# A two-layer gated cross-attention kernel on one core: Layer 0's expert rows weighted on GpSimd, second products feature by token, new orders

## The reference, cut to what matters

```python
scores = xf @ Wr + br                                    # 8 experts, best 2 kept
router_weights = softmax(where(mask, scores, -inf))      # [token, expert]
h = gelu(einsum('td,edp->etp', xf, W1) + b1[:, None, :]) # 512 hidden features
y = einsum('etp,epd->etd', h, W2) + b2[:, None, :]
out = einsum('te,etd->td', router_weights, y)
```

## Time and profile before

| | |
|---|---|
| median of 3 runs | 4908.51 us |
| profiled execution | 4911.92 us |
| its span | 4910.1 us |
| busy: PE, DVE, ACT, POOL | 87%, 86%, 82%, 27% |
| granted TensorE clock, mean | 0.955 |
| DMA | 332.13 MB, mean 68 GB/s |

### The profile page before, as it was taken

One profiled execution on the slowest core, in us unless ns is written; L12 is line 12 of the kernel. 1 busy time (PEld: TensorE's weight loads), 2 busy tenths in 40 slices (PEclk: granted clock), 3 DMA queues, 4 the chain that ended last, 5 costly groups with the idle time before them and its releaser, 6 DMA issues. The chain is left out here.

```text
span 4910.1 us, 108232 instructions
## 1 busy us (share of the span) xinstructions
PE 4268.7 (87%) x33307; PEld 2101.1 (43%) x33862; DVE 4203.5 (86%) x22712; ACT 4014.6 (82%) x5260; POOL 1312.9 (27%) x2809
## 2 busy tenths in 40 slices
PE   5879779999798999889889999997999799998775
PEld 2435235453443535344443535444353444534222
DVE  5478998989989898998989899898989989888782
ACT  2558778989798898879879898997989699898774
POOL 3121222232223223222322333232232223122121
PEclk7889999999999999999999999999999899999887
DMA  5332232323233233323323332332333233131110
GB/s 133 77 81 64 64 69 62 79 63 80 56 77 78 60 74 72 77 59 78 79 48 77 70 88 61 77 83 53 72 73 83 53 76 76 44 70 34 36 29 21
DMA packets 356926, 332.13 MB, mean 68 GB/s; under 512 B 102659, under 2 KB 313750, under 8 KB 356310
## 3 DMA queue, kind: packets, MB, share of 16 engines
q1 hardware_dynamic: 356310, 324.86, 28.7%
HBM read 217.55 MB, written 107.13 MB: 66 GB/s over the span
## 5 line engine op out<-in xcount | busy, mean ns | idle before, releaser
L991 DVE MAX8 cand<-s 128x8 f32<-128x67 f32 (+1 forms) x12288 | 1974.9, 220 | 106.2 <-ACT s L943 92.0
L962 ACT ACTIVATE prob<-wide 128x1024 f32<-128x1024 f32 (+1 forms) x1792 | 1780.8, 1025 | 209.8 <-PE wide L656 80.9
L1077 DVE TENSOR_REDUCE part<-score 128x1 f32<-128x512 f32 x1536 | 1017.9, 677 | 213.7 <-PE score L610 134.4
L656 PE MATMUL wide<-q,k_att 128*128 128x256 bf16 (+1 forms) x6656 | 1008.8, 277 | 78.5 <-ACT prob L962 25.0
L702 PE MATMUL att<-prob,v 128*9 128x256 f32 (+1 forms) x14336 | 1044.8, 383 | 12.6 <-ACT prob L962 7.3
L943 ACT ACTIVATE s<-wide 128x1024 f32<-128x1024 f32 (+1 forms) x1024 | 844.7, 842 | 137.9 <-PE wide L630 130.9
L952 ACT ACTIVATE below<-wide 128x1024 bf16<-128x1024 f32 (+1 forms) x832 | 819.6, 1025 | 100.8 <-PE wide L656 95.9
L656 PEld LDWEIGHTS wide<-q,k_att 128*128 128x128 bf16 (+1 forms) x6656 | 557.8, 99 | 531.0 <-ACT prob L962 182.7
L610 PE MATMUL score<-k_scan,q 128*128 128x512 bf16 x1313 | 501.3, 393 | 189.7 <-DVE part L1077 114.5
L1309 POOL TENSOR_SCALAR flag<-cand,ends 128x24 bf16<-128x24 f32 x512 | 185.6, 363 | 1636.4 <-DVE ends L1016 1518.7
L678 PE MATMUL wide<-below,minus_ident 128*128 128x512 bf16 x1515 | 474.0, 388 | 137.0 <-ACT below L952 62.7
(11 more groups left out here) (169 smaller groups left out, 5257.2 us busy)
## 6 DMA issues: line engine op xcount, KB each, us to landing
k_scan<-k_stack SPq DMA_DIRECT2D x512, 150.1 KB, 3.3
k_stack<-split_b SPq DMA_DIRECT2D x576, 128.0 KB, 2.7
k_att<-k_stack SPq DMA_DIRECT2D x384, 192.0 KB, 3.6
ctxT<-in_ctx_dram SPq DMA_DIRECT2D x32, 800.5 KB, 5.8
q_stack<-split_b SPq DMA_DIRECT2D x192, 64.0 KB, 2.1
q<-q_stack SPq DMA_DIRECT2D x128, 96.0 KB
self_stack<-split_b SPq DMA_DIRECT2D x192, 64.0 KB, 2.0
k_self<-self_stack SPq DMA_DIRECT2D x64, 96.0 KB
```

The lines of the kernel that those rows point to most:

```text
L656: r = tensor.matmul(ps[0:kc, j * S:(j + 1) * S], m.k_att[kn % 3][:, j, c0:c0 + kc], rows[:, j, :], start=(j % 2 == 0), stop=(l == 0), skip ...
L962: scalar.activation(pr[0:kc, :], ps[0:kc, :], ACT.Exp, scale=SCALE).then_inc(sem["wide_done"], 1)
L991: i = vector.max(cand[:, :, c], s[:, KCUT[c]:KCUT[c + 1]])
L1077: vector.tensor_reduce(m.part[:, QT * hh + qt, c:c + 1], score[i % 2][:, :], AX.X, ALU.max).then_inc(sem["score_max"], 1)
```

## The change

Layer 0's second product is turned: w_2 is the weight operand and hid the moving one, so a result stands feature by token (128x256), and the two experts of a pair accumulate into the same bank before DVE adds it to v_acc with one plain addition. Because a token is now a column, the routing weight can't be a per-partition scalar: the eight rows of weights are written to DRAM (gate_out), read back spread over all partitions (gate_in, 128x8x256), and POOL multiplies each expert's hid rows by them (v_gate). At the end two transposes (v_turn) put the sum back token by feature into small, and x_add.v reads it there. The biases are mixed in the turned form as well. hid has four buffers instead of two. w_1 and w_2 are no longer resident: SP loads each expert's 256 KB of each into a ring of four for every batch (w_in). All five orders are new; n0 starts two steps earlier, z_score two later.

```diff
+HIDS = 4
+WBUF = 4
-                  (m.w_1[:, :, :], a["L0_ffn_W1"].rearrange("e d f -> d e f")),
-                      (m.w_2[:, e_, :, :], a["L0_ffn_W2"][e_, :, :].rearrange("(t p) d -> p t d", p=P))]
...
                     elif name == "v_w1":
-                        ps = fill(name, *key)
+                        ps, n = fill(name, *key), E * b + e
+                        q.wait_ge(w_in[n % WBUF], 32 * (n // WBUF + 1))
...
                     elif name == "v_w2":
-                        b, e = key
+                        b, pair = key
                         ps = claim(name, *key)
-                        q.wait_ge(sem["wide_done"], after("v_gelu", b, e))
-                        for t in range(QT):
+                        for e in (2 * pair, 2 * pair + 1):
+                            q.wait_ge(sem["gated"], after("v_gate", b, e))
                             for k in range(PT):
-                                r = tensor.matmul(ps[:, t * D:(t + 1) * D], hid[:, k, t * P:(t + 1) * P],
-                                                  m.w_2[:, e, k, :], start=(k == 0), stop=(k == PT - 1))
+                                r = tensor.matmul(ps[:, 0:S], w_2[:, k, :], hid[:, k, :], start=(e % 2 == 0 and k == 0),
+                                                  stop=(e % 2 == 1 and k == PT - 1))
+                    elif name == "v_turn":
+                        q.wait_ge(sem["v_added"], after("v_add", b, E // 2 - 1))
+                        turned(ps, lambda t: flat(m.r["v"].acc)[:, t * P:(t + 1) * P])
...
                     elif name == "v_add":
-                        for t in range(QT):
-                            y, w = small[:, t * D:(t + 1) * D], r.one[:, t, e:e + 1]
-                            i = vector.scalar_tensor_tensor(r.acc[:, t, :], y, w, r.acc[:, t, :], ALU.mult, ALU.add)
+                        vector.tensor_tensor(acc, small[:, 0:S], acc, ALU.add).then_inc(sem["v_added"], 1)
...
+                    elif name == "v_gate":
+                        q.wait_ge(sem["wide_done"], after("v_gelu", b, e))
+                        q.wait_ge(gate_in, 16 * (b + 1))
+                        gpsimd.tensor_tensor(hid[:, :, :], hid[:, :, :], m.gate_rows[:, e:e + 1, :].to_broadcast([P, PT, S]),
+                                             ALU.mult).then_inc(sem["gated"], 1)
...
+                    elif name == "w_in":
+                        if n >= WBUF:
+                            q.wait_ge(sem["small_full"], after("v_w2", (n - WBUF) // E, (n - WBUF) % E // 2))
+                        sync.dma_start(m.w_1[n % WBUF][:, :], a["L0_ffn_W1"][e, :, :]).then_inc(w_in[n % WBUF], 16)
+                        sync.dma_start(m.w_2[n % WBUF][:, :, :],
+                                       a["L0_ffn_W2"][e, :, :].rearrange("(t p) d -> p t d", p=P)).then_inc(w_in[n % WBUF], 16)
+                    elif name == "gate_out":
+                        q.wait_ge(sem["turned"], after("rw_copy", "v", b))
+                        sync.dma_start(d.gates[b, :, :], m.mixT["v"][0:E, :]).then_inc(gate_out, 16)
+                    elif name == "gate_in":
+                        q.wait_ge(gate_out, 16 * (b + 1))
+                        sync.dma_start(m.gate_rows[:, :, :], d.gates[b:b + 1, :, :].to_broadcast([P, E, S])).then_inc(gate_in, 16)
```

More of the change, by code:

```diff
@@ L85 @@
     pe="""
[L86 to L90, removed]
@@ L106 @@
[L106 to L110, removed]
+        rw_turn.v z_score w_k.0 mix_bias.v c1*2 pv.1 s_1 z_score s_1 z_score cut_add*2 n0 c1 n0 c1*2 n0 s_1 pv.1*2
@@ L111 @@
+        cut_add n0 pv.0 cut_add z_v c1 n0 u_turn.0 w_v.1 n0 c1 o_turn.0 n0 c1 z_qk route.z c1 z_qk n0 s_1*2 pv.1*2
+        cut_add n0 cut_add o_proj.0 w_v.1 s_1 n0*2 s_1 flag cut_add pv.1 rw_turn.z cut_add n0 c1 mix_bias.z z_moe
+        ln_turn.v c1 pv.1 c1*2 route.v n0 s_1*2 row_turn.0 pv.1 cut_add n0 pv.1 cut_add z_moe s_1 z_score n0 s_1
+        pv.1 flag cut_add n0 pv.1 cut_add v_w1 n0*2 v_w1""",
     act="""
-        exp_1 v_gelu*2 w_k_out.0 rw_copy.v c1_out mix_start.v c1_out cut*2 exp_1*2 c1_out*2 cut exp_1 row_minus.2
@@ L165 @@
+        k_scan.0*2 split_out.w_k.1 rows_out.0 k_scan.0 k_scan.1 k_att.0 x_out rows_in.0 k_scan.1 k_att.0*2 q_in.1
+        k_att.0 rows_out.1 k_att.1 rows_in.1 k_att.1 k_scan.1 k_scan.0 q_in.0 split_out.w_k.1*2 k_att.1 k_scan.1
+        split_out.z_qk k_scan.0 k_att.0 split_out.z_qk""",
 )
@@ L289, in streams @@
         of(f"{name}.z_qk", name, [("z_qk", b, n) for b in batches for n in range(2)])
-    for name in ("v_w1", "v_gelu", "v_w2", "v_add"):
+    for name in ("w_in", "v_w1", "v_gelu", "v_gate"):
         of(name, name, [(b, e) for b in batches for e in range(E)])
+    for name in ("v_w2", "v_add"):
+        of(name, name, [(b, pair) for b in batches for pair in range(E // 2)])
+    for name in ("gate_out", "gate_in", "v_turn"):
+        of(name, name, [(b,) for b in batches])
     for kind in "01vz":
@@ L365, in build @@
     smalls = T.number("pe", "small", ("b_o", "ln_turn", "row_turn", "u_turn", "o_turn", "o_proj", "route", "v_w2", "z_v",
-                                      "flag", "rw_turn", "mix_bias"))
+                                      "flag", "rw_turn", "mix_bias", "v_turn"))
     ctx = ExitStack()
@@ L422, in build @@
         m.below = [sb(f"below{n}", [P, HG * S], BF16) for n in range(2)]
-        m.hid = [sb(f"hid{n}", [P, PT, S]) for n in range(2)]
+        m.hid = [sb(f"hid{n}", [P, PT, S]) for n in range(HIDS)]
         m.u, m.rec = sb("u", [P, S]), sb("rec", [P, QT, HG])
@@ L444, in build @@
         d.rows = [dram(f"rows{l}", (B, 3, G, HG * QT, P), BF16) for l in range(3)]
+        d.gates = dram("gates_of_batch", (B, E, S))
         def semaphore(name):
@@ L453, in build @@
         prep_in, weights_in = semaphore("prep_weights_in"), semaphore("weights_in")
+        w_in = [semaphore(f"expert_weights_in{n}") for n in range(WBUF)]
+        gate_out, gate_in = semaphore("gates_out"), semaphore("gates_in")
         x_in = [semaphore(f"x_in{n}") for n in range(5)]
@@ L509, in small_drain @@
                 return "z_v_out", key
+            if name == "v_turn":
+                return "x_add", ("v", *key)
             if name == "rw_turn":
@@ L931, in _ @@
                         q.wait_ge(sem["small_full"], after("mix_bias", *key))
-                        if b:
+                        if b and kind == "v":
+                            q.wait_ge(sem["small_full"], after("v_turn", b - 1))
+                        elif b:
                             q.wait_ge(sem["x_done"], after("x_add", kind, b - 1))
@@ L1197, in _ @@
                         elif kind == "v":
-                            q.wait_ge(sem["v_added"], after("v_add", b, E - 1))
-                            vector.scalar_tensor_tensor(flat(x), flat(m.r["v"].acc), m.gates[:, 2:3], flat(x), ALU.mult,
+                            q.wait_ge(sem["small_full"], after("v_turn", b))
+                            vector.scalar_tensor_tensor(flat(x), small[:, 0:QT * D], m.gates[:, 2:3], flat(x), ALU.mult,
                                                         ALU.add).then_inc(sem["x_done"], 1)
@@ L1236, in _ @@
                             if kind == "v":
-                                q.wait_ge(sem["v_added"], after("v_add", b - 1, E - 1))
+                                q.wait_ge(sem["small_full"], after("rw_turn", kind, b - 1))
                             else:
```

209 lines of the change are left out of this document (111 added, 98 removed), and 2 rows, old and new, of the table sp.

## The result

The changed kernel takes 4991.86 us (median of 4 executions, 4984.09 to 4994.21) beside 4910.1 for the kernel before in the same session (4906.88 to 4914.14): a ratio of 1.0163 [1.0149, 1.0177], slower by 82 us and outside the range of the prediction. The profiled execution took 4994.21 us (span 4992.4), at a mean granted clock of 0.951 against 0.955.

What follows compares the result with a forecast made beforehand. PE was taken as the only bound in the experts' stretch. PE's 16 x -0.6 = -10 and start's -6 took the profiled 4911.9 to 4896, less 3.4 for the median: 4893 us; own range 4880 to 4912, wide range 4838 to 4952.

Steps and rivals of the forecast that it cites:

- Orders: New engine orders: interlocking unreadable from the trace, bounds 16.8 us per round either way, taken as 0.
- What bounds the kernel: Experts' 72 us stretch: PE alone bounds, 97% busy; a microsecond off PE there shortens the round by one.
- Second products, v_turn, biases: PE work per batch: second products save 0.8 us, transposes add 0.4, mixing biases saves 0.2; in all -0.6 us.
- DVE: Multiply-adds replaced by four additions save 3.0 us per batch where DVE is not the bound; counted as 0.
- POOL: Eight gates of 1.90 us per batch; about 2 us spare at the tightest place of PE's order; costed at 0.
- The gate's way: Two dependent DMAs through DRAM, covered by some 20 us of PE words before the first v_w2; 0.
- Weights: Per-batch weight loads in the experts' stretch fit barely; 0, or +32 us in all if late twice per batch.
- Start: Fewer initial weight loads let SP issue first keys and k_scan earlier; bounds 0 to 9 us, taken as 6 saved.
- C: Rival: gates wait behind POOL's marks, stopping PE 2.6 us per batch; +42, 4935 us; chance 0.30 together with late weights.
- A: Rival: new orders give back a fifth of PE's idle time, 54 us in all; 4839 us; chance 0.22.
- B: Rival: PE's saving turns into waiting for ACT's drains, only part of the start remains; 4904 us; chance 0.12.
- The port rule: VectorE and GpSimd lock a shared port during gates: estimated 1.2 us per batch, at most 4912 us; left out of the sum.

Runs made afterwards that it cites:

- before_late: Kernel before with only the first two second products (and their v_add) moved later, four hid buffers, w_2 holding four experts: 4962.9 us, period 281.1 us.
- old_single_light: New products in the orders of before, one expert per bank, gates through DRAM in first batch only, 8-element gate multiplies, weights loaded once: 4985.6 us, period 275.7.
- old_pair_light: As old_single_light, but two experts in one bank, each pair where its second product stood: 5052.8 us, period 280.5.
- swap: Kernel after with one pair of PE words exchanged at the head of the experts' stretch (second n0 and second v_w1): 4973.7 us, ratio 1.0126, period 279.7.
- light_early: As light, with the first pair's second product moved from 238 to 224 us after x_add.v: 5101.4 us, period 284.1.
- no_reload: Kernel after with expert weights loaded once for the ring's four slots and never again: 4958.2 us, ratio 1.0097, period 280.6.
- light: As no_reload, with gates crossing DRAM in the first batch only and gate multiplies of 8 of 1024 elements: 5046.8 us (11 repeats), period 280.6.

## Why the prediction was wrong

*The step that failed* is "Orders". I wrote "I take 0, the nearest row being a round of the old order with the same words", because the experts' words "cover the same part of the string". Words and their number were the same; the places were not. The strings stood in the diff: the first product came 18 us later and eight pieces became four. The term measured 4.7 us a round in place of 0, some 66 us over the 14 rounds. It was shown both ways: before_late puts such a loss into the kernel before, old_single_light takes it out of the new layout, and old_pair_light brings it back by joining the pieces alone. Within the orders of after themselves only 1.1 us of it were given back (swap); light_early made it worse. That the rest of after's loss is the pieces', too, rests on its equal size in the old orders (4.8 and 5.0 us) and on the waits shown; it was not taken out there. What the last two rounds lose beyond 4.7 each, some 11 us together, was not taken apart.

*What bounds the kernel.* "In the stretch that the change touches PE alone is the bound" was half of it. PE was 97% busy there because its second products lay in ACT's and DVE's waits. PE time taken out of such a place isn't a saving but a gap. PE's idle time was also smaller than I read: the row of the 276.1 us round has 2087 matmuls beside 2116 weight loads, so about 29 records are missing. After's rows are nearly whole. One of them at the same full clock as the earlier trace rows:

```profile
2573.55:2854.53 280.98, 264.73 (x2056) 126.56 (x2054) 249.83 (x1398) 250.20 (x330) 100.17 (x182) 1.00 0.38 91
```

Before has 1.0 us more work (16.0 - 14.6 of second products, 0.71 - 0.69 of mix_bias, less 0.38 of v_turn), so I estimate 265.7 busy and 10.4 idle, not 16.8. After idles 281.0 - 264.7 = 16.3: 5.9 more idle less 1.0 of work is the 4.9 by which this round is longer than 276.1.

*Second products, v_turn, biases:* second products 14.6 us a round for 15.2 forecast, v_turn 0.38 for 0.40. mix_bias is 0.69 us, not the 0.48 of a v_w1 matmul among others: its two records alone take that long (L765, 0.69 at 3072.47), and nothing was saved on 0.71. PE's work fell by 1.0 us where 0.6 was forecast: nearly right as work, and nothing of it reached the period of after.

*DVE:* v_add at 0.42 us each, 1.7 for 4.8; the saving counted at 0, right. DVE's busy time in the round stayed at 249.8 even so; 1.6 us of it went to one instruction beside a gate (below, the port rule).

*POOL:* the gate took 2.36 us, not the 1.90 of the earlier trace rows. "About 2 us are spare" at the tightest place held in its letter, since PE never waits for a gate in after. It asked the wrong question: not whether the new order waits for gates, but what it gave up in order not to.

*The gate's way:* 0 by "some 20 us of words lie between", and these words cover it. Where the products stood before it would have cost 7.3 us of waiting.

*Weights:* 0 in the rounds, right (no_reload); PE waited once for them in the whole run, 1.2 us.

*Start:* SP's queue, which answers to the earlier trace rows, has its first keys and first k_scan earlier, by 8.9 and 3.9 us:

```profile
21.39 12.65 SPq L1452 DMA_DIRECT2D k_stack<-split_b  x12
...
49.31 7.73 SPq L1475 DMA_DIRECT2D k_scan<-k_stack  x3
```

Yet the first x_add.v came at 264.6 in both and the second 6.9 us later than before. The 6 us didn't arrive. What takes them was not tried.

*The rivals:* C had the sign, by another mechanism: PE waited for no gate in the whole run, and its 4935 was too little. A's direction was wrong: the orders gave nothing back. B had the principle, that a saving of PE can turn into waiting, but only down to zero.

*The port rule.* The routing's instruction of 8 columns is as long as in the earlier trace rows, v_one here once 1726 ns:

```profile
L1269 DVE SCALAR_TENSOR_TENSOR v_one<-iota,v_atf,v_e x32: 212/218/1726, 210.6 to 4514.0; 128x8 f32<-128x8 f32 x32
L1269 DVE SCALAR_TENSOR_TENSOR v_two<-iota,v_atf,v_e x32: 212/218/1291, 210.9 to 4515.3; 128x8 f32<-128x8 f32 x32
```

The Trainium skill ("SBUF — State Buffer", Who interferes with whom) has VectorE and GpSimd share a port pair as a lock, and the trace agrees in these lengths. But all the long ones lie beside layer 1's expert sum, its additions (L1351) and once its multiply (L1346), none beside a gate; before, too, they lie beside that sum's additions (L1326) and not, as I wrote, beside the 1.9 us multiply (L1321). What does stand beside a gate is one short instruction of the normalization, in 13 of the 16 batches; after, then light:

```profile
L1083 DVE TENSOR_SCALAR rstd<-mv x64: 168/169/2122, 25.4 to 4920.4; 128x2 f32<-128x2 f32 x64
L1083 DVE TENSOR_SCALAR rstd<-mv x64: 169/170/171, 25.4 to 4974.5; 128x2 f32<-128x2 f32 x64
```

That is 1.6 us of DVE a round, near the 1.2 that I estimated. As a price of this change it is refuted: light takes it away with nearly all of the gates' reads, and its period of 280.6 is that of after.

The prediction's own test says the same: a period that moves by more than 1.5 us without a wait for hid or for w means that the orders made the time.

## What to carry to other kernels

Where an order is written out by hand and three engines are nearly full, ask of each instruction that moves not only what it will wait for, but which wait of its own engine it was covering; look at what follows it in the old order. Small pieces of work that need nothing just then are worth more as fillers than their busy time says, and joining two of them, or putting a latency in front of them, can cost more than it saves. A trace's missing records make a full engine look idle: compare the number of products with the number of weight loads before reading idle time as room.

## What was not expected of the hardware

GpSimd's multiply of 128x1024 f32 takes 1.90 us where the other factor is 8 numbers in each partition, each read 128 times, and 2.36 us where it is a row of 256 numbers in each partition, read 4 times (L1361, 128 times, mean 2355 ns).

The same 30 us of the stretch's start in before, in the round of after shown above and in the round of after just ahead of it:

```profile
3021.20:3051.20 30.00, 28.90 (x195) 18.29 (x194) 28.51 (x156) 25.95 (x41) 11.95 (x21) 1.00 0.11 25
```
```profile
3064.50:3094.50 30.00, 26.09 (x152) 13.62 (x145) 25.54 (x134) 24.76 (x41) 16.50 (x20) 0.94 0.23 66
2783.60:2813.60 30.00, 24.78 (x151) 12.96 (x152) 26.28 (x136) 25.12 (x41) 17.23 (x20) 1.00 0.25 66
```

The granted clock is 0.94 in the round shown, so part of it ran at the lower level of 1.2 GHz, behind PE's waits of 1.42 and 1.51 us. The round ahead has the same two waits (1.41 and 1.51 us) at 1.00, so these waits alone don't decide it. Nor does the clock make the loss: that round is 281.0 us long, the one shown 280.4.
